# Layer 1 of a two-layer graph network on one core: the load of the next tile's own rows is issued ahead of the store of the finished tile

## The chip, the cores and the metric

The kernel runs on one core of a Trainium2 chip. A core has a matrix engine (PE in the profile, its weight loads PEld), a vector engine (DVE), a scalar engine (ACT), a general engine (POOL, here the one that issues gathers) and a sync engine (SP, here the one that issues plain loads and stores). All transfers run on the core's 16 DMA engines. The metric is the time of one execution on the device in microseconds (us), as the median of several runs.

## What is computed

Two layers of message passing over 6250 nodes with 512 features and 106,250 edges, each followed by a layer norm. What matters here is layer 1:

```
msg   = h[dst] @ W_neigh.T + b_neigh
neigh = segment_sum(msg, src, num_segments=n) / max(deg, 1)
out   = relu(h @ W_self.T + b_self + neigh)
x     = h + out
y     = layernorm(x) * ln_gamma + ln_beta
out   = layernorm(h + y)
```

## The kernel before

The nodes are cut into T = 49 tiles of 128. The sums over the neighbours of layer 1 are taken first over rows, and multiplied by the weights afterwards: 882 chunks of 128 edges each, 18 chunks (HALF) to a round, and 49 rounds.

For each chunk POOL issues one gather (line 562) of 128 rows of a table in memory into one slot of a ring of 12 (RING; the profile calls eight of them `rows` and four `flat`). A gather waits until PE has finished with the chunk 12 before it (semaphore `s_mm`). PE multiplies the chunk by a matrix of zeros and ones (three matmuls at line 1278, `ps<-rows` or `ps<-flat`, the second operand being `onehot` or `spot`), and DVE adds the product to the sum of its tile (line 1078, `acc<-acc,ps`).

Between the chunks of a round the engines finish one tile and begin another, by a step number k that runs with the chunks from 0 to 17. In the round of tile j ("front"), PE turns the tile's own rows at k = 0 (`turn_own`, line 1473, `ps<-ident,zeros` or `ps<-ident,g_loc`), and multiplies them by `w_b` and the mean of the neighbours by `w_a` (`ps<-w_ab,flat`). DVE evicts the product at k = 15 (line 1138), and takes the first norm's sum at k = 16. For the tile before, j - 1 ("back"), DVE does the rest: at k = 5 `outer_sums` (line 1116), which is the last reader of that tile's own rows and raises `s_y`; at k = 11 the factors of the last norm. Then ACT writes the result (line 1759, `edges<-flat,nb_b,rs_b`) and raises `s_out`.

The tile's own rows lie in one of two buffers, `own1[0]` and `own1[1]`; the profile calls them by the storage that they lie in, `zeros` and `g_loc`. SP loads them (line 455, from `h_scratch`, 256 KB) in `far_load(j, slot)`, which first reads the tile's number (line 451) and then waits until `outer_sums` of tile j - 2 is done (`s_y` at least j - 1). SP stores the result (line 465, `out<-edges`, 256 KB) in `far_store(j)`, which reads the tile's number (line 463) and waits for `s_out` at least j + 1. SP does nothing else in layer 1, and does it in the order in which it is written.

PE waits for the load at k = 0 of its round. Its order is written out by hand, so a wait there holds all later matmuls of the chunks too.

Of the kernel before, what the change touches and what calls it, by code (L numbers as in the profile page):

```python
# [18 lines left out]
def gnn_two_layers(nc, x, src, dst, w_l_t, b_l, w_r_t, w_self_t, b_self, w_neigh_t, b_neigh, gamma, beta, out):  # L19
# [6 lines left out]
    T = -(-N // P)  # L26
# [43 lines left out]
    with ctx:  # L70
# [127 lines left out]
        r = [flat[:, (4 + k) * D:(5 + k) * D] for k in range(2)]  # L198
# [155 lines left out]
        def _(sp):  # L354
# [91 lines left out]
            def far_load(j, slot):  # L446

                if isinstance(j, int) and j == T - 1:
                    rows_at = h_dram[(T - 1) * P:T * P, :]
                else:  # L450
                    tile = sp.value_load(order[0:1, ds(j, 1)], min_val=0, max_val=T - 2)
                    rows_at = h_dram[ds(tile * P, P), :]
                if not (isinstance(j, int) and j < 2):
                    sp.wait_ge(s_y, j - 1)
                sp.dma_start(own1[slot], rows_at).then_inc(s_own1[slot], 16)

            def far_store(j):

                if isinstance(j, int) and j == T - 1:
                    sp.wait_ge(s_out, T)  # L460
                    sp.dma_start(out[(T - 1) * P:N, :], res1[0:LAST, :]).then_inc(s_st1, 16)
                else:
                    tile = sp.value_load(order[0:1, ds(j, 1)], min_val=0, max_val=T - 2)
                    sp.wait_ge(s_out, j + 1)
                    sp.dma_start(out[ds(tile * P, P), :], res1).then_inc(s_st1, 16)
            far_load(0, 0)
            far_load(1, 1)
            far_store(0)
            far_load(2, 0)
            with sp.Fori(1, (T - 3) // 2) as c:  # L470
                for r in range(2):
                    far_store(2 * c - 1 + r)
                    far_load(2 * c + 1 + r, (1 + r) % 2)
            far_store(T - 4)
            far_load(T - 2, (T - 2) % 2)
            far_store(T - 3)
            far_load(T - 1, (T - 1) % 2)
            far_store(T - 2)
            far_store(T - 1)
            sp.wait_ge(s_st1, 16 * T)  # L480
# [1334 lines left out]
```

## Time and profile before

| | |
|---|---|
| Median of 3 runs | 2754.21 us (2752.51 to 2757.79) |
| The profiled execution | 2761.44 us, of which the span from first to last instruction is 2759.7 us |
| PE, DVE, POOL busy | 83%, 80%, 66% of the span |
| Mean granted clock of PE | 0.915 of full speed |
| Gathers of layer 1 | first at 1571.94 us, last at 2708.20 us |

The profile is of one execution, which took 7.2 us more than the median of the others. Layer 1 is the stretch from about 1570 us to the end. POOL's busy time doesn't count the 0.30 us or so between two gathers in which its sequencer gets the next one ready.

### The profile page before, as it was taken

The page shows a single profiled execution, that of the slowest core. Times are in us where ns is not written, and L with a number is a line of the kernel's source. Part 1 is how long each engine was busy: PE and PEld are TensorE (multiplying, and loading weights), DVE is VectorE, ACT ScalarE, POOL GpSimd, SP SyncE. Part 2 cuts the span into 40 slices and gives each one's busy share as a digit, 9 for nine tenths or more (in the row PEclk, how much of TensorE's full clock was granted, in tenths as well). Part 3 has the DMA queues.
Part 4 walks back from the last instruction along what each step waited for, and adds up shares of the span by engine and source line. Part 5 has one row for each costly group of instructions (what it writes and reads, how often), then busy time and mean ns, then how long its engine had stood idle before and what let it go on. Part 6 is the DMA issues. An engine that isn't in the chain of part 4 may idle for free.

```text
span 2759.7 us, 53159 instructions
## 1 busy us (share of the span) xinstructions
PE 2288.0 (83%) x9900; PEld 1018.5 (37%) x9900; DVE 2197.9 (80%) x5204; ACT 1404.7 (51%) x3569; POOL 1817.2 (66%) x1938
## 2 busy tenths in 40 slices
PE   2389889999999999999888778888888888888885
PEld 1123234444444444444334323333333333333332
DVE  5889888998989889998588667777777777777774
ACT  6300056666676666664234445555555555555552
POOL 2666777777777777777111277777777777777771
PEclk8579999999999999999999889998898889888887
DMA  9766777787777777777456677778777777777774
GB/s 301 207 168 192 234 218 229 227 236 227 229 235 230 228 236 228 232 233 237 136 152 177 217 210 228 231 230 231 233 230 230 225 222 231 226 225 228 229 200 86
DMA packets 211934, 600.32 MB, mean 218 GB/s; under 512 B 35752, under 2 KB 36582, under 8 KB 211876
## 3 DMA queue, kind: packets, MB, share of 16 engines
q0 software_dynamic: 144800, 476.45, 61.1%
q1 hardware_dynamic: 66596, 121.95, 13.6%
q10 hardware_dynamic: 480, 1.28, 0.2%
q8 instruction: 20, 0.33, 0.1%
q14 instruction: 38, 0.31, 0.0%
HBM read 535.25 MB, written 64.28 MB: 217 GB/s over the span
## 4 chain that ended last, share of the span: by engine, by line
PE 47%; DVE 16%; DMA 14%; issue 11%; ACT 4%; DVEq 4%; SPq 1%; POOL 1%; ACTq 0%; POOLq 0%
PE ps L1278 44%; DMA rows<-table,idx_ring 5%; DMA g_loc<-h_scratch 3%; DVE where L1017 3%; DMA zeros<-h_scratch 3%; DVE acc L1004 3%; DVE onehot L991 2%; DVEq L998 2%; PE ps L1473 1%; DMA table<-rows 1%; DVE acc L1078 1%; POOL rows L546 1%; PE ps L1480 1%; ACT edges L1759 1%; ACT put L1714 1%
## 5 line engine op out<-in xcount | busy, mean ns | idle before, releaser
L546 POOL DMA_INDIRECT rows<-table,idx_ring x928 | 907.1, 978 | 319.7 <-issue 200.4
L1278 PE MATMUL ps<-rows,onehot 128*128 128x512 f16 (+1 forms) x3378 | 731.4, 332 | 205.6 <-DVE acc L1004 75.2
L1278 PE MATMUL ps<-w_ab,flat 128*128 128x512 f32 x1568 | 854.0, 646 | 15.2 <-ACT flat L1737 14.7
L1078 DVE TENSOR_TENSOR acc<-acc,ps 128x513 f32 x882 | 607.2, 688 | 287.4 <-PE ps L1278 181.5
L562 POOL DMA_INDIRECT rows<-table,idx_ring x590 | 568.8, 964 | 210.9 <-issue 119.3
L1278 PEld LDWEIGHTS ps<-rows,onehot 128*128 128x128 bf16 x3378 | 317.2, 103 | 651.0 <-issue 231.7
L1635 ACT ACTIVATE spot<-iota_node,flat 128x128 f16<-128x128 f16 x832 | 340.0, 479 | 241.0 <-DVE flat L857 241.0
L1278 PE MATMUL ps<-where,put 128*128 128x442 bf16 x1664 | 436.8, 353 | 29.1 <-DVE where L1017 28.7
L1017 DVE TENSOR_SCALAR where<-iota_chunk,cw_ring 128x884 bf16<-128x884 f16 x832 | 427.2, 522 | 7.2 <-PE ps L1278 0.2
L1004 DVE TENSOR_TENSOR acc<-acc,ps 128x513 f32 x464 | 318.3, 686 | 80.4 <-PE ps L1278 42.9
L1647 ACT ACTIVATE put<-spot,flat 128x128 f16<-128x128 f16 x832 | 265.7, 390 | 164.2 <-PE ps L1278 152.9
L562 POOL DMA_INDIRECT flat<-table,idx_ring x292 | 281.4, 964 | 93.9 <-issue 65.4
L1278 PEld LDWEIGHTS ps<-w_ab,flat 128*128 128x128 f32 x1568 | 262.2, 200 | 178.8 <-issue 94.1
L991 DVE TENSOR_SCALAR onehot<-iota_node,loc_ring,rows 128x128 bf16<-128x128 f16 x928 | 312.5, 337 | 15.4 <-DMA rows<-table,idx_ring 12.8
L1714 ACT ACTIVATE put<-iota_node,loc_ring 128x128 f16<-128x128 f16 x882 | 271.5, 387 | 3.8 <-DVE idx_ring L1059 3.8
L1278 PE MATMUL ps<-rows,spot 128*128 128x512 f16 (+1 forms) x1176 | 225.7, 311 | 26.5 <-DMA rows<-table,idx_ring 14.8
L1278 PEld LDWEIGHTS ps<-where,put 128*128 128x128 f16 x1664 | 122.7, 97 | 228.5 <-issue 88.9
L1278 PEld LDWEIGHTS ps<-rows,spot 128*128 128x128 bf16 x1176 | 103.3, 98 | 208.7 <-issue 101.6
L527 POOL COPY acc<-zeros 128x513 f32 (+1 forms) x49 | 31.8, 648 | 208.9 <-ACT flat L1677 208.9
L1745 ACT ACTIVATE where<-flat,nm_a 128x512 bf16<-128x512 f32 x49 | 35.4, 722 | 255.6 <-DVE nm_a L1146 255.6
L1741 ACT ACTIVATE flat<-ps 128x512 f32<-128x512 f32 x49 | 29.3, 598 | 222.0 <-PE ps L1480 222.0
L1654 ACT ACTIVATE flat<-ps 128x512 f32<-128x512 f32 x49 | 29.3, 597 | 201.4 <-PE ps L1421 201.4
(234 smaller groups left out, 2037.7 us busy)
## 6 DMA issues: line engine op xcount, KB each, us to landing
rows<-table,idx_ring POOLq DMA_INDIRECT x1518, 3.8
table<-rows SPq DMA_DIRECT2D x77, 257.0 KB, 3.5
xr_scratch<-edges SPq DMA_DIRECT2D x49, 256.0 KB
rows<-xr_scratch SPq DMA_DIRECT2D x49, 256.0 KB, 3.3
h_scratch<-rows SPq DMA_DIRECT2D x49, 256.0 KB, 2.0
edges<-in_x SPq DMA_DIRECT2D x48, 256.0 KB, 4.6
out<-edges SPq DMA_DIRECT2D x48, 256.0 KB
acc<-in_x SPq DMA_DIRECT2D x6, 1792.0 KB, 17.9
```

What stands on the lines that cost most here:

```text
L546: nc.gpsimd.indirect_dma_start(out=rows[:, k % GB, :], out_offset=None, in_=tables[layer][:, :], in_offset=bass.IndirectOffsetOnAxis(ap=id ...
L562: nc.gpsimd.indirect_dma_start(out=rows1[k % RING], out_offset=None, in_=tables[1][:, :], in_offset=bass.IndirectOffsetOnAxis(ap=idx_ring[ ...
L991: V.tensor_scalar(onehot[:, k % SB, :], iota_node[:], loc_ring[:, k:k + 1], rows[:, k % GB, 2 * D:2 * D + 2].bitcast(f32), ALU.is_equal, A ...
L998: tile = dve.value_load(g_tile[layer][0:1, ds(U // g * i + q, 1)], min_val=0, max_val=T - 1)
L1004: V.tensor_tensor(tile_acc, tile_acc, part, ALU.add).then_inc(s_acc, 1)
L1017: V.tensor_scalar(where_bf[:, (2 * half + j) % PB, 0:CHUNKS[1]], iota_chunk[:, 0:CHUNKS[1]], cw_ring[:, j, 0:1], cw_ring[:, j, 1:2], ALU.i ...
L1078: V.tensor_tensor(tile_acc, tile_acc, part, ALU.add).then_inc(s_acc, 1)
L1278: return nc.tensor.matmul(*args, skip_group_check=True, **kw)
L1635: last = nc.scalar.activation(spot[:, at + k, :], iota_node[:], ACT.Abs, scale=value[:, ds(col + k, 1)], bias=shift_v[:, ds(col + k, 1)])
L1647: nc.scalar.activation(puts_of[g % 3][:, k, :], spot[:, at + k, :], ACT.Relu, scale=-1.0, bias=value[:, ds(col + k, 1)]).then_inc(s["put"], 1)
L1714: last = nc.scalar.activation(apart[:, at + k, :], iota_node[:], ACT.Abs, bias=loc_ring[:, HB * slot + k:HB * slot + k + 1])
L1745: nc.scalar.activation(junk, rr, ACT.Square, bias=nm_a[:, p:p + 1], accum_out=sq_a[:, p:p + 1]).then_inc(s_sqa, 1)
```

## The change

SP's program in layer 1 is written anew. Where it had `far_store(m)` and behind it `far_load(m + 2)`, it has `far_load(m + 2)` and behind it `far_store(m)`. Loads, stores, their sizes, their buffers and what each of them waits for are as they were.

```
             far_load(0, 0)
             far_load(1, 1)
-            far_store(0)
-            far_load(2, 0)
-            with sp.Fori(1, (T - 3) // 2) as c:
+            with sp.Fori(1, (T - 1) // 2) as c:
                 for r in range(2):
-                    far_store(2 * c - 1 + r)
-                    far_load(2 * c + 1 + r, (1 + r) % 2)
-            far_store(T - 4)
-            far_load(T - 2, (T - 2) % 2)
+                    far_load(2 * c + r, r)
+                    far_store(2 * c - 2 + r)
+            far_load(T - 1, (T - 1) % 2)
             far_store(T - 3)
-            far_load(T - 1, (T - 1) % 2)
             far_store(T - 2)
             far_store(T - 1)
```

On SP, the loop over the rounds stands so before; `[waits s_out]` is the wait for a finished result and `[waits s_y]` the wait for a free buffer:

```order
L463 TENSOR_LOAD order
L463 ISA x2
L465 ISA [waits s_out]
L465 DMA out<-edges 128x512
L451 ISA
L451 TENSOR_LOAD order
L451 ISA x2
L455 ISA [waits s_y]
L455 DMA g_loc<-h_scratch 128x512
```

And so in the same place of the changed kernel, for the same half of the loop:

```order
L451 ISA
L451 TENSOR_LOAD order
L451 ISA x2
L455 ISA [waits s_y]
L455 DMA g_loc<-h_scratch 128x512
L463 ISA
L463 TENSOR_LOAD order
L463 ISA x2
L465 ISA [waits s_out]
L465 DMA out<-edges 128x512
```

The load with its wait for `s_y` now stands ahead of the wait for `s_out`; nothing stands between the store before and the load but the reading of the tile's number. At the program's end, before:

```order
L463 TENSOR_LOAD order
L463 ISA x2
L465 ISA [waits s_out]
L465 DMA out<-edges 128x512
L455 DMA zeros<-h_scratch 128x512 [waits s_y]
L463 TENSOR_LOAD order
L463 ISA x2
L465 ISA [waits s_out]
L465 DMA out<-edges 128x512
L461 DMA out<-edges 106x512 [waits s_out]
```

and now:

```order
L455 DMA zeros<-h_scratch 128x512 [waits s_y]
L463 TENSOR_LOAD order
L463 ISA x2
L465 ISA [waits s_out]
L465 DMA out<-edges 128x512
L463 TENSOR_LOAD order
L463 ISA x2
L465 ISA [waits s_out]
L465 DMA out<-edges 128x512
L461 DMA out<-edges 106x512 [waits s_out]
```

The last load has moved ahead of the store of tile T - 3; the last three stores keep their order.

## Rows read from the trace of the kernel before

**Rows 1.** Chain that ended last, 1946 to 2158 us: shares by line.

```profile
by line: PE ps L1278 47.7%; DMA zeros<-h_scratch 14.8%; DMA g_loc<-h_scratch 9.0%; issue 8.0%; PE ps L1473 4.1%; DVE acc L1078 3.7%; ACT edges L1759 2.7%; PE ps L1480 2.1%; ACT put L1714 1.6%; SPq L451 1.6%; SPq L465 1.4%; DVEq L1078 1.1%; 
```

**Rows 2.** Waits, 1946 to 2684 us: us in total, times, longest.

```profile
PE ps L1473 <- DMA zeros<-h_scratch: 49.2, 16, 4.2
PE ps L1473 <- DMA g_loc<-h_scratch: 41.0, 16, 3.9
```

**Rows 3.** Timeline of SP: start, duration; stores and loads at three places.

```profile
1962.48 0.36 SPq L465 DMA_DIRECT2D out<-edges  x1
...
2077.83 0.35 SPq L465 DMA_DIRECT2D out<-edges  x1
2079.02 0.33 SPq L455 DMA_DIRECT2D zeros<-h_scratch  x1
...
2684.39 0.36 SPq L465 DMA_DIRECT2D out<-edges  x1
```

**Rows 4.** Groups of POOL's gathers, 1573 to 1945 us: busy, mean ns, idle before.

```profile
L562 POOL DMA_INDIRECT rows<-table,idx_ring x197 | 189.6, 962 | 60.0 <-issue 39.9 <-PE ps L1278 17.1 <-DVE idx_ring L1059 3.0
L562 POOL DMA_INDIRECT flat<-table,idx_ring x96 | 93.2, 971 | 29.3 <-issue 21.3 <-PE ps L1278 6.7 <-DVE idx_ring L1059 1.2
```

**Rows 5.** The same groups, 2158 to 2710 us.

```profile
L562 POOL DMA_INDIRECT rows<-table,idx_ring x280 | 270.9, 968 | 98.9 <-issue 55.3 <-PE ps L1278 41.5 <-DVE idx_ring L1059 2.1
L562 POOL DMA_INDIRECT flat<-table,idx_ring x140 | 134.1, 958 | 47.6 <-issue 34.0 <-PE ps L1278 11.4 <-DVE idx_ring L1059 2.1
```

**Rows 6.** Timeline of POOL, the last gathers: idle before each in brackets.

```profile
2702.39 0.94 POOL L562 DMA_INDIRECT rows<-table,idx_ring  x1 [6.85 <-PE ps L1278]
...
2706.80 0.94 POOL L562 DMA_INDIRECT rows<-table,idx_ring  x1 [0.97 <-PE ps L1278]
2708.20 0.94 POOL L562 DMA_INDIRECT rows<-table,idx_ring  x1 [0.46 <-issue]
```

**Rows 7.** Gathers (line 562) in two stretches: length, busy, (xcount).

```profile
1570.00:1822.00 252.00, 190.35 (x197) 0.89 0.78 229
...
1570.00:2158.00 588.00, 445.25 (x463) 0.89 0.79 230
```

**Rows 8.** DVE's adds (line 1078) in the same two stretches.

```profile
1570.00:1822.00 252.00, 132.07 (x192) 0.89 0.78 229
...
1570.00:2158.00 588.00, 310.55 (x451) 0.89 0.79 230
```

**Rows 9.** Timeline of DVE: ends of `outer_sums` in two rounds, and the last add.

```profile
2069.00 0.08 DVE L1116 DVE_READ_ACCUMULATOR flat<-flat,rs_a,zeros 128x1 f32 x1
...
2675.57 0.08 DVE L1116 DVE_READ_ACCUMULATOR flat<-flat,rs_a,zeros 128x1 f32 x1
...
2721.45 0.69 DVE L1078 TENSOR_TENSOR acc<-acc,ps 128x513 f32 x1 [0.23 <-DVE acc L1078]
```

**Rows 10.** Timeline of PE: the turn in two rounds, idle before it in brackets.

```profile
2086.04 0.69 PE L1473 MATMUL ps<-ident,zeros 128*128 128x128 f32 x2 [4.16 <-DMA zeros<-h_scratch]
...
2699.64 0.69 PE L1473 MATMUL ps<-ident,zeros 128*128 128x128 f32 x2 [11.10 <-DMA zeros<-h_scratch]
```

**Rows 11.** Line 455 (the loads), 1570 to 2684 us; then one piece of the chain.

```profile
DMA to landing us min/median/max: 3.6/5.9/7.1
...
2685.58 14.01 DMA zeros<-h_scratch
```

**Rows 12.** Waits for gathers, 1571 to 1945 us.

```profile
PE ps L1278 <- DMA rows<-table,idx_ring: 44.8, 32, 16.9
```

**Rows 13.** All engines in two stretches: PE, PEld, DVE, ACT, POOL busy (x), clock, DMA share, GB/s.

```profile
1570.00:1946.00 376.00, 296.12 (x1203) 128.18 (x1203) 265.42 (x602) 195.20 (x483) 284.49 (x295) 0.89 0.79 230
...
2200.00:2684.00 484.00, 405.57 (x1623) 181.44 (x1622) 359.47 (x836) 264.59 (x651) 360.46 (x374) 0.88 0.78 224
```

**Rows 14.** Timeline of PE after a short stop: start, duration.

```profile
1807.15 2.83 PE L1278 MATMUL ps<-rows,onehot 128*128 128x512 f16 x9
1810.01 1.82 PE L1278 MATMUL ps<-w_ab,flat 128*128 128x512 f32 x2
```

## The prediction

> **What bounds the kernel now.** I read the chain of what ended last first. In the middle of layer 1 it runs again and again through the load of a tile's own rows: 14.8% and 9.0% of a stretch [rows 1]. That looks like a quarter of layer 1, some 270 us, and the reader should distrust it, because a chain only says what was last, not what comes next once it is gone. So the second view is the list of waits: from 1946 to 2684 us PE stood still for these loads 32 times, 90.2 us in all, 2.8 us a round [rows 2]. The third is what POOL does meanwhile. From 1573 to 1945 us its 293 gathers have 89.3 us of idle time before them, 0.305 us each, with a mean length of 0.965 us [rows 4]: a gather every 1.27 us with never a real wait, whatever PE does. Eighteen of them make 22.9 us, and a round cannot be shorter than that. Measured rounds, from the store at 1962.48 us to the one at 2684.39 us, 31 rounds, are 23.29 us long [rows 3]. Thus PE waits 2.8 us a round and all but some 0.4 us of it would have been spent waiting for gathers.
>
> What ties the two together is the ring of 12. The counts of gathers issued and of adds begun differ by 5 at 1822 us and by 12 at 2158 us [rows 7, 8]. While the distance is 5 or less, PE follows the gathers and POOL never stops. Each wait for a load adds to the distance, and PE and DVE don't quite get it back within a round; at 12 the ring is full and POOL itself is held. So two things are to be had: POOL's stops, and the distance at the end.
>
> **The change part by part.** It adds and removes no instruction that costs anything; 47 loads (tiles 2 to 48) move ahead of one store each.
>
> *Where the load goes.* Its own wait is for `outer_sums`. In the round shown that ends at 2069.08 us [rows 9], and the load goes out at 2079.02 us, 1.19 us behind the store of the finished tile [rows 3]. PE came to the turn at 2086.04 - 4.16 = 2081.88 us [rows 10]. The load takes 3.6 to 7.1 us, 5.9 in the middle [rows 11]. Issued at about 2069.5 us it lands at 2073 to 2077 us, 5 to 9 us before PE asks. At POOL's pace the 13 chunks from k = 5 to the next k = 0 take 13 x 1.27 = 16.5 us, so the cover is no thinner. The wait of 2.8 us a round should be gone. One load took 14.0 us [rows 11]: issued at 2676 instead of 2685.58 us it would land at 2690, where PE came at 2699.64 - 11.10 = 2688.54 us [rows 9, 10]; about 1.5 us of wait would be left of 11.10.
>
> *What PE and DVE do then.* Their own round is 23.29 - 2.8 = 20.5 us, against POOL's 22.9. They gain 2.4 us a round on the gathers until the distance is back at its floor of 4 or 5; it starts there, and without the wait nothing drives it to 12. POOL is then never held.
>
> *Term 1, POOL's stops.* From 2158 to 2710 us, 420 gathers have 98.9 + 47.6 = 146.5 us idle before them [rows 5]. At 0.305 us each, the value of the early stretch, 128.1 us are its own; 18.4 us are stops. Three of the last gathers hold 6.85 + 0.97 + 0.46 - 0.9 = 7.4 us of these [rows 6]; they follow the 14.0 us load. The other 11.0 us are the usual ones.
>
> *Term 2, the distance at the end.* The last gather goes out at 2708.20 us [rows 6], the last add starts at 2721.45 us [rows 9]: 13.25 us later. At the floor, 4 or 5 gathers of 1.27 us apart are 5 to 6.5 us, and I take 6.5, since loads, stores and gathers share the DMA engines: 6.75 us less. With no gain in distance at all it would be 0, with 5 us it would be 8.2.
>
> *Term 3, the tail.* From the last add to the end there are 38 us with no gathers, a chain of turns, products and norms for the last two tiles. The loads of these tiles also go out earlier, but there the turn waits for what DVE and ACT do first, so I take 0; the bound is the length of one usual wait, 2.8 us.
>
> *The store.* It now stands behind the load in SP's order. The load's wait (`outer_sums` of tile m) is always over before the result of tile m exists, so the store isn't held; it loses the 1.2 us that the load stood behind it at most, and ACT, which must not overwrite the result before it is stored, comes back a round later. Cost 0.
>
> **The sum.** Against the profiled execution: 2761.44 - 18.4 - 6.75 = 2736.3 us. Against the median of the runs, which I take to be without the 14.0 us load (it cost 7.4 us on POOL, and the profiled execution is 7.2 us over the median): 2754.21 - 11.0 - 6.75 = 2736.5 us. I take 2736.
>
> **What speaks against it.** In the early stretch, where POOL is never held, PE waited 44.8 us in 32 times for gathers, 16.9 of it for the first [rows 12], so about 0.9 us each; load and store push gathers back when they move. Those waits stay, since the load still moves its 256 KB. In the sum they stand as the floor of the distance. The Trainium skill ("DMA: Bandwidth & Descriptors", section "Issuing engines are not separate DMA queues") says that transfers of all issuing engines interleave on the same 16 DMA engines; by it a moved load moves its disturbance too, and the trace agrees that the DMA engines are 79% busy in the stretch at the floor [rows 13]. That becomes a rival below.
>
> **The rivals.**
>
> *A, the forecast:* the load is hidden, POOL is never held, the distance ends at 4 to 6 gathers. 2729 to 2745 us. Chance 0.74.
>
> *B, late gathers in place of the late load:* the load now moves at k = 6 to 10, apart from the store, so gathers land late twice a round. If each time costs PE as much as half the wait it had, PE gets no slack, the distance stays near 12, and only part of POOL's stops goes: half of 11.0 is 5.5, giving 2754.2 - 5.5 = 2749 us; with the distance mended but the stops left, 2754.2 - 6.75 = 2747.5 us. For it: [rows 12]. Against: the early stretch had both transfers on top of each other and POOL didn't stop once. Chance 0.14.
>
> *C, the wait was hidden anyway:* something else holds PE for the same 2.8 us, DVE's adds above all, and PE's 20.5 us is no true round. DVE is busy 359.47 of 484 us, 74%, in the late stretch [rows 13], so I give it little. 2752 to 2757 us. Chance 0.05.
>
> *D, slower, by the clock of PE:* right after a stop PE is at the lower of its two clocks (1.2 GHz), where three chunks take 2.83 us, 0.94 each, and two products 1.82 us [rows 14]. A round all at that clock would be 18 x 0.94 + 4 x 1.82 + about 2 for the turns = 26.2 us, 2.9 more than now, over 47 rounds 136 us more. If PE follows each gather closely it idles a little before each chunk instead of long once a round. The clock must fall so far that PE's round passes 23.4 us, about three quarters of it at the lower level. Against: the early stretch, where PE already follows the gathers, has a clock of 0.89, the late one 0.88 [rows 13]. From that point on the time is above 2760 us. Chance 0.03.
>
> *E, more than forecast:* the gathers themselves, 0.965 us in the mean, get shorter where less collides, or the tail gives its 2.8 us: below 2729 us. Chance 0.04.
>
> **How the numbers follow.** 0.2% of 2754 is 5.5 us, about what a measurement can tell from no change; below 2748.7 us counts as faster. All of A and E and about 0.08 of B lie there: 0.86. Within: the rest of B and most of C: 0.10. Slower: D and a little of C: 0.04. The range: A and E down to 2728, B up to 2748, which leaves out C, D and about half of B's upper end.
>
> **What the profile of the changed kernel would show.** SP: each load some 9 us before the store. PE: no waits of over 1 us at line 1473 for a load from `h_scratch`. POOL: idle before a gather 0.305 us to the end, about 269 us for all 882; the last gather at about 2690 us. Distance: 4 to 6 gathers at 2158 and at 2607 us; last add 5 to 7.5 us after the last gather. The tail from the last add to the end unchanged, 38 us. The prediction is wrong if PE's waits for gathers grow by as much as those for loads shrink, if POOL is still held late in the layer, or if the granted clock falls below 0.8.

## The result, and the profile after

The changed kernel takes 2777.36 us in the median of 5 runs (2775.2 to 2789.21), the kernel before 2753.97 us beside it: a ratio of 1.0089, with a 95% interval of 1.0064 to 1.0114. It is slower by 23 us, where 18 us less were forecast. The profiled execution took 2783.33 us, its span is 2781.6 us, and PE's mean granted clock rose from 0.915 to 0.925.

The chain of the changed kernel, 1946 to 2158 us, by line; it answers to [rows 1]. Lines after the change are four lower than before (1274 is 1278 before, 1733 is 1737, 558 is 562); in the experiments an edit further up can move them again, so that ACT's copy of the turned rows is line 1733, 1735, 1739 or 1741 there.

```profile
by line: PE ps L1274 51.8%; issue 15.0%; ACT put L1710 7.3%; DVE acc L1074 6.2%; ACT where L1741 3.5%; DVEq L1074 2.8%; ACT flat L1733 2.3%; PE ps L1476 2.1%; ACTq L1722 1.9%; ACT flat L1727 1.4%; DVE flat L1138 1.0%; DVEq L1059 1.0%; DVE f
```

The loads are gone from it, and ACT has come in: one-hots (1710), the spread (1741), the copy of the turned rows (1733). The waits of the same kernel, 1946 to 2684 us, answer to [rows 2]:

```profile
PE ps L1274 <- DVE acc L1074: 89.3, 108, 2.0
...
PE ps L1274 <- ACT flat L1733: 39.4, 31, 1.6
```

The 90.2 us of waits for loads are gone entirely. Waits for DVE and ACT are 128.7 us, where they were 31.5 us before:

```profile
PE ps L1278 <- DVE acc L1078: 26.4, 48, 0.9
...
PE ps L1278 <- ACT flat L1737: 5.1, 6, 1.6
```

In sum PE waits 128.7 us instead of 121.7, so the waits were not removed but moved. SP's timeline answers to [rows 3]:

```profile
2136.80 0.35 SPq L465 DMA_DIRECT2D out<-edges  x1
2150.95 0.33 SPq L455 DMA_DIRECT2D g_loc<-h_scratch  x1
2160.57 0.36 SPq L465 DMA_DIRECT2D out<-edges  x1
```

The load goes out 9.6 us ahead of the next store, as foretold, and lands 3.9 us later in the median of 1946 to 2684 us. Gathers and adds in two stretches answer to [rows 7, 8], gathers first:

```profile
1570.00:1822.00 252.00, 191.50 (x198) 0.87 0.79 229
1570.00:2158.00 588.00, 442.49 (x454) 0.90 0.78 225
```

```profile
1570.00:1822.00 252.00, 129.97 (x189) 0.87 0.79 229
1570.00:2158.00 588.00, 304.43 (x443) 0.90 0.78 225
```

The distance is already 9 at 1822 us, where it was 5, and 11 at 2158 us. In the 24 rounds from the 21st to the 45th first mean of DVE a round takes 23.90 us, before 23.33. The ring of slots fills sooner and POOL goes at the pace of PE and DVE for longer.

**One round, before and after.** I laid the rounds on top of each other by DVE's first mean (L1146 before, L1142 after), from which ACT's work follows at the same distances. The round before is one of the 11 of the 24 whose product starts no later than in the changed kernel; one with a longer wait stands further down. Before:

```profile
2550.29 0.15 DVE L1146 TENSOR_SCALAR nm_a<-sum_a 128x1 f32<-128x1 f32 x1
...
2552.12 1.11 PE L1473 MATMUL ps<-ident,zeros 128*128 128x128 f32 x4 [2.29 <-DMA zeros<-h_scratch]
...
2553.03 2.74 PE L1278 MATMUL ps<-rows,onehot 128*128 128x512 f16 x9
...
2555.27 0.58 ACT L1737 ACTIVATE flat<-ps 128x512 f32<-128x512 f32 x1
...
2555.89 1.13 PE L1278 MATMUL ps<-w_ab,flat 128*128 128x512 f32 x2
...
2557.32 1.10 PE L1278 MATMUL ps<-w_ab,flat 128*128 128x512 f32 x2
...
2558.26 0.60 PE L1278 MATMUL ps<-rows,onehot 128*128 128x512 f16 x3
```

After:

```profile
2187.85 0.61 PE L1274 MATMUL ps<-rows,onehot 128*128 128x512 f16 x3 [0.58 <-DVE acc L1074]
...
2188.32 0.63 PE L1469 MATMUL ps<-ident,zeros 128*128 128x128 f32 x4
...
2188.93 0.14 DVE L1142 TENSOR_SCALAR nm_a<-sum_a 128x1 f32<-128x1 f32 x1
...
2190.13 0.61 PE L1274 MATMUL ps<-rows,onehot 128*128 128x512 f16 x3 [0.46 <-DVE acc L1074]
...
2192.74 1.04 PE L1274 MATMUL ps<-rows,onehot 128*128 128x512 f16 x3 [1.99 <-DVE acc L1074]
...
2193.90 0.58 ACT L1733 ACTIVATE flat<-ps 128x512 f32<-128x512 f32 x1
...
2194.53 2.08 PE L1274 MATMUL ps<-w_ab,flat 128*128 128x512 f32 x2 [0.76 <-ACT flat L1733]
...
2197.33 1.84 PE L1274 MATMUL ps<-w_ab,flat 128*128 128x512 f32 x2
...
2199.00 0.60 PE L1274 MATMUL ps<-rows,onehot 128*128 128x512 f16 x3
```

Two things are to be seen. First, the own product (`ps<-w_ab,flat`) starts 5.60 us after the first mean in both: 2555.89 - 2550.29, and 2194.53 - 2188.93. It waits for ACT's copy of the turned rows, which ACT reaches 4.98 and 4.97 us after the mean, behind the spread, a batch of one-hots and the mean of the neighbours. In this round the wait for the load lay beside that. Second, PE's speed. Before, the turn and the three chunks behind the load's wait run at the lower clock (1.11 us for the turn against 0.63 us), and at the products PE is at the higher one: 1.13 us for two. After, the turn is fast, PE stops for 1.99 and 0.76 us later, and the lower clock lies over two pairs of products: 2.08 and 1.84 us. From the first product to the chunk behind the second pair it is 2.37 us before and 4.47 us after.

Not every round before is like this. In 13 of the 24 the load comes so late that the product starts later than in any round of the changed kernel, as here, 7.29 us after the mean:

```profile
2082.34 0.15 DVE L1146 TENSOR_SCALAR nm_a<-sum_a 128x1 f32<-128x1 f32 x1
...
2086.04 1.11 PE L1473 MATMUL ps<-ident,zeros 128*128 128x128 f32 x4 [4.16 <-DMA zeros<-h_scratch]
...
2089.63 1.20 PE L1278 MATMUL ps<-w_ab,flat 128*128 128x512 f32 x1
```

So I cut each of the 24 rounds in three: from the first mean to the first product, from there to the turn of the mean (line 1480 before, 1476 after), and from there to the next first mean. The means, in us:

| run | to the first product | products to the turn of the mean | to the next mean | round |
|---|---|---|---|---|
| before | 5.93 | 3.52 | 13.88 | 23.33 |
| changed | 5.43 | 4.61 | 13.86 | 23.90 |

The early load does give something: 0.50 us a round. The lower clock over the products takes 1.09 us. In the first piece the changed kernel goes by ACT's chain alone: the product starts 5.60 and 5.24 us after the mean in turns. At the higher clock the second piece takes 2.8 us, as e12_warm_k2 shows below, and the three pieces would add up to 22.1 us, below POOL's 22.9.

### The profile page after: what moved, and what is told of

Its sections match the earlier page's. It is cut to its first block, busy times and chain, and to the rows that moved or that the text cites. A ratio compares the mean times of both kernels' runs of the same rounds, so it can differ in the third digit from the quotient of the medians.

```text
span 2781.6 us, 53188 instructions
## 1 busy us (share of the span) xinstructions
PE 2296.8 (83%) x9900; PEld 1001.8 (36%) x9900; DVE 2198.0 (79%) x5204; ACT 1404.6 (50%) x3569; POOL 1827.4 (66%) x1938
## 4 chain that ended last, share of the span: by engine, by line
PE 47%; DVE 19%; issue 13%; DMA 8%; ACT 7%; DVEq 5%; ACTq 1%; POOL 1%; POOLq 0%; SPq 0%
PE ps L1274 45%; DMA rows<-table,idx_ring 5%; DVE where L1013 3%; ACT put L1710 3%; DVE acc L1000 3%; DVE acc L1074 3%; DVE onehot L987 2%; DVEq L994 2%; ACT where L1741 1%; DVEq L1074 1%; DMA table<-rows 1%; ACT flat L1733 1%; DMA flat<-table,idx_ring 1%; POOL rows L542 1%; PE ps L1476 1%
## 5 line engine op out<-in xcount | busy, mean ns | idle before, releaser
L1274 PE MATMUL ps<-w_ab,flat 128*128 128x512 f32 x1568 | 889.0, 669 | 61.6 <-ACT flat L1733 61.5
L1274 PE MATMUL ps<-rows,onehot 128*128 128x512 f16 (+1 forms) x3378 | 713.7, 324 | 248.3 <-DVE acc L1000 79.1
L1274 PEld LDWEIGHTS ps<-rows,onehot 128*128 128x128 bf16 x3378 | 306.7, 100 | 705.6 <-issue 218.9
L1274 PE MATMUL ps<-rows,spot 128*128 128x512 f16 (+1 forms) x1176 | 227.4, 313 | 26.9 <-DVE acc L1074 12.4
```

What stands on the lines that cost most here:

```text
L1274: return nc.tensor.matmul(*args, skip_group_check=True, **kw)
```

## The experiments

The theories, as the expectations name them. **Theory 1:** the wait for the load lay beside ACT's chain, so its removal gives little; the stop moves on, and the low clock that follows stops now lies over the products. **Theory 2:** the load at its new place disturbs the gathers. **Theory 3** (for the kernel before): the load's wait itself is what costs. **Theory E** is about the end of the kernel.

All ratios are to the kernel before on the same chip. "Round" is the mean of the 24 rounds named above, "product" the mean of a matmul `ps<-w_ab,flat` in 2060 to 2620 us, "lag" the time from the start of the last gather to the start of the last add; all three are of the profiled execution.

| run | median, us | ratio (95% interval) | round, us | product, ns | lag, us |
|---|---|---|---|---|---|
| before | | 1 | 23.33 | 675 | 13.3 |
| changed | 2777.36 | 1.0089 (1.0064 to 1.0114) | 23.90 | 722 | 16.8 |
| e1_held | 2775.6 | 1.0016 (0.9975 to 1.0057) | 23.89 | 724 | 19.0 |
| e10_held_fill | 2740.35 | 0.9950 (0.9930 to 0.9970) | 22.96 | 635 | 17.2 |
| e2_warm | 2737.7 | 0.9914 (0.9885 to 0.9943) | 22.87 | 632 | 18.5 |
| e12_warm_k2 | 2735.61 | 0.9935 (0.9911 to 0.9959) | 22.81 | 634 | 17.0 |
| e3_no_load | 2782.26 | 1.0074 (1.0051 to 1.0097) | 23.89 | 723 | 19.1 |
| e5_before_fill | 2736.16 | 0.9933 (0.9915 to 0.9952) | 22.88 | 635 | 16.3 |
| e4_turned_early | 2744.38 | 0.9930 (0.9910 to 0.9950) | 22.87 | 635 | 19.3 |
| e6_before_turned_early | 2741.17 | 0.9955 (0.9935 to 0.9975) | 23.18 | 680 | 14.2 |
| e7_swap | 2741.7 | 0.9944 (0.9922 to 0.9966) | 22.94 | 640 | 17.5 |
| e11_held_long | 2775.28 | 1.0082 (1.0060 to 1.0104) | 23.89 | 668 | 16.5 |
| e8_both | 2736.39 | 0.9937 (0.9916 to 0.9959) | 22.90 | 629 | 17.5 |
| e16_spread | 2720.38 | 0.9880 (0.9857 to 0.9904) | 22.75 | 632 | 6.4 |

**e3_no_load: does the transfer itself disturb?**

```
-                sp.dma_start(own1[slot], rows_at).then_inc(s_own1[slot], 16)
+                n = P if isinstance(j, int) and j < 2 else 1
+                sp.dma_start(own1[slot][0:n, :], rows_at[0:n, :]).then_inc(s_own1[slot], 16)
```

> The changed kernel, with the loads of tiles 2 to 48 cut to one row of 128, so the output is not the reference's from tile 2 on; all waits and semaphores stay. Theory 1: nothing of the transfer matters, 2770 to 2782 us. Theory 2 (transfer disturbs gathers): the loss is gone, 2735 to 2757 us.

With 47 of 49 loads cut to one row the kernel is as slow as the changed one, ratio 1.0074, and its rounds are as long, 23.89 us, in the same three pieces: 5.43, 4.60 and 13.87 us. Theory 2 is out. Its trace shows one thing more. The first 11 rounds take 22.98 us each, POOL's pace, with PE waiting for gathers and products of 642 ns (1640 to 1880 us); after these the kernel falls into rounds of 23.4 and 24.2 to 24.6 us in turns and stays there up to the 45th. So the changed kernel can go as I forecast, and doesn't keep to it. In its own trace the slow rounds are there from the fourth on. What tips it from one into the other is not shown.

**e2_warm and e12_warm_k2: PE's stops filled with work.** Of the changed kernel; e12 has 0 in place of 4.

```
-                elif k in (3, 4, 6, 7):
-                    own_product(j, (3, 4, 6, 7).index(k))
+                elif k in (2, 3, 4, 6, 7):
+                    if k in (2, 3):
+                        if not (isinstance(j, int) and j == 0):
+                            pe.wait_ge(s_ev, j)
+                        for _ in range(8 if k == 2 else 4):
+                            mm(ps[:, 1, :], iota_node[:], iota_chunk[:, 0:D], start=True, stop=True)
+                    if k > 2:
+                        own_product(j, (3, 4, 6, 7).index(k))
```

> The changed kernel, with 8 filler matmuls of 128x512 behind chunk 2 and 4 behind chunk 3 of each round, into the bank that the own product overwrites; the output is unchanged. They fill PE's two longest stops (1.99 us for DVE, 0.76 us for ACT). Theory 1: PE stays at its higher clock over the products, rounds shrink from 23.9 us towards 23.0, the time is 2735 to 2757 us. Theory 2: 2777 us or more, since only work was added.

> The changed kernel with the 8 fillers behind chunk 2 only; PE's stop for ACT ahead of the own product stays. Theory 1 (it is the sum of stops that brings the clock down, ahead of the products): with the longest stop filled the clock stays up and the products stay near 635 ns, ratio 0.990 to 0.997. If the stop just ahead of the products matters: products near 700 ns, ratio above 1.002.

Added work makes the kernel faster: 0.9914 and 0.9935. The groups of PE's products in 2060 to 2620 us, for the changed kernel, then e2_warm (count, busy us, mean ns, idle us before them):

```profile
L1274 PE MATMUL ps<-w_ab,flat 128*128 128x512 f32 x376 | 239.0, 722 | 30.0 <-ACT flat L1733 30.0
```

```profile
L1274 PE MATMUL ps<-w_ab,flat 128*128 128x512 f32 x396 | 217.9, 632 | 2.0 <-ACT flat L1739 1.9
```

At 632 ns the products are at the higher clock throughout, and the 30.0 us of waits for ACT are nearly all filled. e12 puts nothing into the stop for ACT, which shrinks to 3.7 us all the same, and its products are as fast, 634 ns: filling the longest stop is enough. From the first product to the turn of the mean it takes 2.78 us in e2 and 2.81 us in e12, where the changed kernel has 4.61; the third piece is 13.87 and 13.92 us. PE is then early enough to wait for gathers.

**e1_held and e10_held_fill: the same wait, empty and filled.** PE waits at the turn for an event of ACT in both (the last two lines added, all that e1 has); e10 has 9 filler matmuls ahead of the turn as well, and ahead of them a wait for DVE's last eviction (`s_ev`), since they write into its bank.

```
             def turn_own(j, p):
+                if not (isinstance(j, int) and j == 0):
+                    pe.wait_ge(s_ev, j)
+                for _ in range(9):
+                    mm(ps[:, 1, :], iota_node[:], iota_chunk[:, 0:D], start=True, stop=True)
                 pe.wait_ge(s_own1[p], ...)
+                if not (isinstance(j, int) and j == 0):
+                    pe.wait_ge(s_da, j)
```

> The changed kernel, with PE made to wait at the turn of a tile's own rows (k = 0) until ACT has taken the spread of the tile before (s_da at least j), an event some 1.3 us after DVE's first mean, close to where the load used to land (1.8 to 2.9 us after it). Theory 1 (the wait for the load lay beside ACT's chain to the own product, and PE's low clock after a stop lay over cheap work; with the load early the stop comes later and the low clock lies over the products): PE's stop is back at the turn, so the time is back at 2750 to 2760 us, faster than the changed kernel's 2777 although a wait was added. Theory 2 (the load at its new place disturbs gathers or their issue): no change, 2775 to 2785 us.

> e1_held with 9 filler matmuls ahead of the turn, the length of PE's stop of 1.88 us there. The wait is as long as in e1_held. Theory 1 (the low clock, not the wait): products fall from 724 to about 635 ns and the ratio to 0.990 to 0.997. If waits alone make the loss: as e1_held, near or above 1.002.

e1 did not do what I expected of it. Its ten times fall into two groups, four from 2746.79 to 2757.28 us and six from 2774.26 to 2786.53 us, and the profiled one is of the upper group; a median over both says little. PE's waits in e1_held, 2060 to 2620 us:

```profile
PE ps L1471 <- issue: 45.2, 24, 1.9
PE ps L1274 <- DVE acc L1074: 30.0, 48, 0.9
PE ps L1274 <- ACT flat L1735: 23.0, 23, 1.2
```

The wait at the turn is 1.9 us, shorter than that for the load; PE then still stops for DVE (0.87 us) and ACT (1.18 us), and in its trace the lower clock lies over the products again (724 ns). Its three pieces are those of the changed kernel, 5.43, 4.60 and 13.87 us: the hold neither cost nor gave anything. With the first of these stops filled, e10 has the same dependency and is faster than before, 0.9950, with products at 635 ns and rounds of 22.96 us. PE works in e10 while it would wait in e1, and the hold at the turn stays: what costs is the low clock, not the wait.

The trace of e1_held tips over as that of e3_no_load does: the first five rounds take 23.04 us, all later ones 23.90. At some 0.9 us a round over some 40 rounds this would be 36 us, an estimate, and the two groups of times lie about 30 us apart. So executions that never tip over would explain the faster group; no trace of one was kept.

**e5_before_fill: the kernel before, its load as late as ever.** As in e10, with 13 matmuls and no hold.

> The kernel before, its load as late as ever, with 13 filler matmuls of 128x512 ahead of the turn of the own rows (some 2.8 us of work at the higher clock, the length of PE's mean wait for the load); the output is unchanged. Theory 1 (what the wait for the load costs is only the low clock after it): the filler takes the place of the stop, the clock stays up, products fall from 677 towards 635 ns, and the time is 2737 to 2750 us although the load is as late as before. Theory 3 (what counts is the wait for the load itself): no gain, 2752 to 2765 us, or slower by the fillers.

0.9933. The products, 2060 to 2620 us, in the kernel before, then in e5:

```profile
L1278 PE MATMUL ps<-w_ab,flat 128*128 128x512 f32 x384 | 226.8, 675 | 4.0 <-ACT flat L1737 3.7
```

```profile
L1278 PE MATMUL ps<-w_ab,flat 128*128 128x512 f32 x391 | 216.5, 635 | 16.3 <-ACT flat L1741 16.2
```

The late load never cost its 2.8 us a round. With PE kept at work until it lands, the kernel before reaches POOL's pace, 22.88 us a round. Waits for ACT rise from 3.7 to 16.2 us: the chain beside the load's wait becomes visible. Theory 3 is out: at the higher clock the 0.50 us a round that the late load did cost are hidden as well, since 22.1 + 0.50 us, an estimate, is still below POOL's 22.9.

**e4_turned_early, e6_before_turned_early and e7_swap: ACT's chain shortened.** e4 is of the changed kernel, e6 the same edit of the kernel before; e7 only swaps the first two calls in the changed kernel.

```
                     mean1_of(front, r)
-                    own_turned(front)
+                    if isinstance(front, int) and front == 0:
+                        own_turned(front)
...
                             spread_a(front, r)
+                            if not (isinstance(front, int) and front == T - 1):
+                                own_turned(front + 1)
```

> The changed kernel, with ACT's copy of the turned own rows (own_turned, line 1733) moved from behind the mean of its own round to right behind the first spread of the round before, ahead of the third batch of one-hots: some 4 us earlier. Theory 1: PE's wait for ACT ahead of the own product goes, and with it the chain that set the round in both kernels; 2735 to 2765 us, with POOL held less. Theory 2: 2775 to 2785 us.

> The kernel before with ACT's copy of the turned rows moved ahead of the third batch of one-hots, as e4 does to the changed kernel. Here the turn itself waits for the late load, so ACT's copy waits too and holds the one-hots. Theory 1 (the load's wait lay beside ACT's chain, and shows once that chain is shortened): smaller gain than e4 had, or a loss: 2745 to 2765 us. If the late load costs nothing at all, the same gain as in e4: a ratio of 0.993.

> The changed kernel with ACT's copy of the turned own rows just ahead of the mean in its own round instead of behind it: 0.7 us earlier for PE, the mean 0.6 us later. Theory 1 (the last wait ahead of the products is ACT's chain): PE's wait of 1.28 us a round for ACT is about halved, rounds 23.9 to about 23.3 us or less, 2745 to 2768 us. If the chain through ACT doesn't set the round: 2775 to 2782 us.

e4 0.9930, e7 0.9944, e6 0.9955. In e4 and e7 PE hardly waits for ACT ahead of the products any more; PE's waits in e7, 2060 to 2620 us:

```profile
PE ps L1274 <- DMA rows<-table,idx_ring: 43.9, 50, 1.9
PE ps L1274 <- DMA flat<-table,idx_ring: 35.3, 37, 2.0
PE ps L1274 <- DVE acc L1074: 14.6, 19, 1.5
PE ps L1274 <- ACT flat L1733: 2.5, 6, 0.8
```

PE waits for gathers now: POOL is the bound, which I had forecast for the changed kernel as it is. Two calls swapped bring it about. The products are at the higher clock here too, 635 and 640 ns, so these two runs don't tell the shorter chain from the clock that comes with it. With the same edit the late load has rounds of 23.18 us (e6) where the early one has 22.87 us (e4). That the early load is of use here is not shown, though: the intervals of the two overlap, and the profiled execution of e6 is the slowest of its eight, 9.6 us over their median.

**e11_held_long: the long stop put back at its old place.**

```
+                if not (isinstance(j, int) and (j == 0 or j > T - 3)):
+                    pe.wait_ge(s_apart, 3 * j + 9)
```

> The changed kernel with PE held at the turn until ACT has made the first half of the third batch of one-hots, 3.07 us after DVE's first mean: one stop of about 3.5 us at the place where the load's wait was, and the load early. Theory 1 (position of the low-clock spell): the clock falls at the turn and is up again at the products; products below 690 ns, 2750 to 2765 us, less than the changed kernel. Against it: as the changed kernel, 2775 to 2785 us.

A miss: 1.0082, rounds of 23.89 us. The products are quicker, 668 ns against 722, as the theory has it. But the hold was too long: the first product starts 2188.39 - 2181.67 = 6.72 us after the mean instead of 5.60. The three pieces show both sides: 6.72, 3.30 and 13.87 us, where the changed kernel has 5.43, 4.61 and 13.86. With the stop and the spell behind it over the turn, 1.31 us are saved at the products, and the hold takes 1.29 us ahead of them. So the place of the spell does decide what it costs the products; no run shows a stop at the turn that is not too long.

**e8_both and e16_spread: what is left.** e8 is e2_warm with e4's edit. e16 is e2_warm with this, where `part_no` is a column of the partitions' numbers:

```
-                V.tensor_copy(idx_ring[:, slot * HB:slot * HB + HB], g_idx[1][:, ds(j * HB, HB)]).then_inc(s_idx, 1)
+                V.tensor_scalar(idx_ring[:, slot * HB:slot * HB + HB], g_idx[1][:, ds(j * HB, HB)], part_no[:], None,
+                                ALU.max).then_inc(s_idx, 1)
```

> The changed kernel with both edits that helped: ACT's copy of the turned rows early, and 8 and 4 filler matmuls behind chunks 2 and 3. Output unchanged. Both alone reached POOL's pace of 22.87 us a round, so theory 1 gives no further gain: a ratio to before of 0.990 to 0.995. If the low clock or ACT's chain still cost something at POOL's pace: below 0.989.

> e2_warm with each index of a gather of layer 1 raised to at least its partition's number, so that unused places of a chunk, which all name row 0, name 128 different rows; the few real indices below 128 are changed too, so the output is slightly off the reference's. Theory E (the last 20 or so gathers, nearly all unused places, land late because all their rows are the same one): the last add comes 5 to 8 us behind the last gather instead of 18.5, and the time falls some 10 us below e2_warm's: ratio 0.986 to 0.990. If the slow landings at the end have another cause: as e2_warm, 0.991.

e8 gives nothing beyond either edit, 0.9937: at POOL's pace neither has anything left to take. e16 gives 0.9880, the fastest of all, 2720.38 us, 16 us below e8 on the same chip; it is no kernel to keep as it stands, since its output is slightly off. The last gather and the last add of e2_warm, then of e16_spread:

```profile
2685.82 0.95 POOL L558 DMA_INDIRECT rows<-table,idx_ring  x1 [0.30 <-issue]
...
2704.31 0.69 DVE L1074 TENSOR_TENSOR acc<-acc,ps 128x513 f32 x1 [1.64 <-PE ps L1274]
```

```profile
2677.60 0.94 POOL L561 DMA_INDIRECT rows<-table,idx_ring  x1 [0.30 <-issue]
...
2684.02 0.69 DVE L1078 TENSOR_TENSOR acc<-acc,ps 128x513 f32 x1 [0.23 <-DVE acc L1078]
```

18.5 us of lag became 6.4 us, the value that I had forecast for the changed kernel. The transfers show why, e2_warm from 2660 to 2695 us, then e16_spread from 2645 to 2680 us (packets and rate; the median time of a gather to landing is the last number):

```profile
DMA packets 1838, 5.72 MB, mean 164 GB/s; under 512 B 338, under 2 KB 338, under 8 KB 1837
...
rows<-table,idx_ring POOLq DMA_INDIRECT x14, 12.9
```

```profile
DMA packets 2675, 8.05 MB, mean 230 GB/s; under 512 B 481, under 2 KB 481, under 8 KB 2674
...
rows<-table,idx_ring POOLq DMA_INDIRECT x19, 3.8
```

## Why the prediction was wrong

**The step that failed** is the one under "What PE and DVE do then": "Their own round is 23.29 - 2.8 = 20.5 us". It subtracts a wait from the round as if nothing else ran during it, and takes PE's speed as given. ACT's chain to the own product ran beside the wait and let the product start no sooner than 5.43 us after the first mean, so that only 0.50 of the 2.8 us could be had; and PE's new stops, for DVE and ACT, brought the lower clock over the products, which took 1.09 us. Waits for DVE and ACT went from 31.5 to 128.7 us in the stretch from 1946 to 2684 us. The round came out at 23.90 us, not 20.5; at the higher clock it would be 22.1, an estimate from the three pieces. The gain of 2.4 us a round on the gathers didn't exist.

**Term 1, POOL's stops (18.4 us less),** rested on that step, and had the wrong sign: the ring fills earlier and a round takes 0.57 us more. Over 48 rounds that would be 27 us, an estimate; 23 us were measured.

**Term 2, the distance at the end (6.75 us less),** rested on it too, and was wrong for a second reason. At the end the last 20 or so gathers land late, which I had taken for one slow load of the profiled execution: every trace but that of e16 has a lag of 13 to 19 us. e16_spread shows the cause: it changes only indices below a partition's number, so the late gathers name a few of the table's first rows over and over (by the code, row 0 for each unused place). Even kernels at POOL's pace have a lag of 16.3 to 19.3 us at the end. The slow load comes back as well, with 12.6 us in the changed kernel and 12.4 in e2_warm. So the 14.0 us load was no accident, and hardly the reason why the profiled execution stood 7.2 us over the median.

**What was right.** *Where the load goes:* all waits for loads vanished from 1946 to 2684 us, and the landing was hidden with room: issued at 2150.95 us, a load of 3.9 us is there 10 us before the turn at 2164.91 us. *The store:* it wasn't held, and it cost nothing. *Term 3, the tail:* from the last add to the end 38.2 us before and 38.5 us after. POOL's pace as the floor of a round was right as well, 22.9 us: seven kernels at 22.81 to 22.96 us reach it, and one, e16, gets just below.

**The rivals.** *B*, late gathers: out, by e3_no_load. *C*, the wait was hidden anyway, had 0.05; its mechanism was half of the truth, though I looked for it in DVE's adds and not in ACT's order. *D*, the clock, had 0.03, the right sign and the wrong form: I made it depend on the mean granted clock falling to where PE's whole round exceeds POOL's. The mean rose, and that the time lies above 2760 us all the same is luck. What counts is which instructions the low spell lies over: on the chain, the piece with the products took 1.09 us more in the mean of 24 rounds, and 2.1 us more in the two rounds shown. The Trainium skill ("TensorE: Matmul & The Clock Gate", section "A second HAM failure mode: psum-queue depth-cycling") describes that short stops of PE between groups of matmuls, with PSUM banks taken in turn, make the clock swing; it has this from another kernel. The traces agree: no stop in the changed kernel's round is over 2.0 us, and its clock falls once a round.

**What stays open.** That the low clock makes the loss is shown by two pairs, changed and e2_warm, e1_held and e10_held_fill, and by the three pieces of the round, of which the one with the products alone grew. That before the change the spell was cheaper because it lay over the turn and three chunks is read from the traces, before, changed and e11_held_long; no run is faster for it. Not shown is why the changed kernel starts at POOL's pace in e3_no_load and e1_held and then tips over into the slower rounds for good, while the kernel before and the filled kernels don't.

## What to carry to other kernels

A wait on the chain is worth its length only if nothing else ends beside it: before taking one out, lay a round's other chains on the same clock and ask which would release the next instruction, here ACT's copy some 5 us after the mean. Do it over many rounds and not for one: the round that I laid beside the other hid that the load did cost 0.50 us in the mean. When PE's short stops bring its clock down, look at which matmuls the slow spell covers, and fill the stop or move it; a few matmuls that nobody needs were worth some 1.5% (e12_warm_k2 at 0.9935 against 1.0089, each to the kernel before), and swapping two calls on ACT about as much (0.9944). A lag that stands at a kernel's end in every trace is no accident; here its cause lay in the data.

## What the runs showed of the hardware

Adding PE work made both kernels faster: 13 matmuls a round in front of a wait, 0.9933, and 8 behind chunk 2, 0.9935. In the round of the changed kernel shown above, the lower clock came behind stops of 0.58, 0.46 and 1.99 us: the chunk behind the third took 1.04 us, against 0.61 us for the ones ahead of it. In the round from 2140.24 us the same chunk behind a stop of 2.00 us still took 0.61 us, and the lower clock came behind the next stop, of 1.17 us. In e1_held it came behind 0.58, 1.88, 0.87 and 1.18 us.

Gathers whose 128 places nearly all name the same row of memory take far longer to land, 12.9 us against 3.8 us in the median, and the DMA engines, busy all the while, move 164 GB/s instead of 230. Loads issued then are slow as well: 12.4 us in e2_warm, where e16_spread has 3.6 us.
